# GpSimd instead of VectorE for the weight-block sums, the third-phase operand sums and the input additions

## What is computed

```
q, k, v = x@Wq, x@Wk, x@Wv ;  a = softmax(q k^T / sqrt(512)) v @ Wp + bp
c   = gelu(a@cW1 + cb1)@cW2 + cb2 + onehot(code)          # 512 -> 2048 -> 512
m   = gelu([a, c]@mW1 + mb1)@mW2 + mb2                    # 1024 -> 2048 -> 512
y   = clip(x + c + m, 0, 1)
z   = layernorm(y + gelu(y@Wd[e]+bd[e])@Wu[e]+bu[e])      # expert e of each sequence
```

## Time and profile before

| | |
|---|---|
| median of 3 runs | 1040.34 us |
| the profiled execution, span from its first to its last instruction | 1039.0 us |
| TensorE busy | 1028.9 us, 4857 matmuls |
| VectorE busy | 792.5 us, 1380 instructions |
| ScalarE busy | 524.4 us |
| GpSimd busy | 7.5 us, 18 instructions |
| mean granted TensorE clock | 0.999 of full speed |

### The profile page before, as it was taken

How to read it: one execution, slowest core, us unless ns; L and a number is a source line. 1 busy time by engine, 2 the same in 40 slices (tenths; PEclk the granted TensorE clock), 3 DMA queues, 4 the chain that set the end, 5 groups by cost and what they waited for, 6 DMA issues and landing times.

```text
span 1039.0 us, 13809 instructions
## 1 busy us (share of the span) xinstructions
PE 1028.9 (99%) x4857; PEld 859.5 (83%) x4857; DVE 792.5 (76%) x1380; ACT 524.4 (50%) x955; POOL 7.5 (1%) x18
## 2 busy tenths in 40 slices
PE   8999999999999999999999999999999999999997
PEld 7899888888888878888889888888888887888886
DVE  5647957767598898887966796677668889887798
ACT  4336875454265443433565487554435644434357
POOL 0000000000000000000000000000000000000001
PEclk9999999999999999999999999999999999999999
DMA  8340211210133272521644122312004322423152
GB/s 205 60 183 21 95 48 41 82 41 21 61 144 121 101 201 83 159 85 49 238 120 118 58 68 82 122 41 81 21 21 162 142 81 104 157 98 109 41 163 81
DMA packets 91006, 101.61 MB, mean 98 GB/s; under 512 B 36830, under 2 KB 71738, under 8 KB 87098
## 3 DMA queue, kind: packets, MB, share of 16 engines
q1 hardware_dynamic: 90848, 100.71, 29.8%
q10 hardware_dynamic: 90, 0.02, 0.0%
HBM read 79.74 MB, written 20.97 MB: 97 GB/s over the span
## 4 chain that ended last, share of the span: by engine, by line
PE 59%; DVE 3%; ACT 1%; issue 1%; DVEq 0%; ACTq 0%
PE bank L224 20%; PE bank L225 20%; PE bank L226 20%; DVE acc L1124 0%; PE bank L462 0%; DVE z_last L1281 0%; DVE w_lo L1018 0%; DVE z_last L1290 0%; ACT gel L833 0%; DVE xp2l L1018 0%; ACT acc L810 0%; DVE hid_lo L1018 0%; ACT xp3h L586 0%; ACT e3h L586 0%; PE bank L376 0%
## 5 line engine op out<-in xcount | busy, mean ns | idle before, releaser
L224 PE MATMUL bank<-hid_hi,w_lo 128*128 128x512 f32 x512 | 200.3, 391 | 0.3
L676 ACT ACTIVATE sbc<-sbc,bias 128x512 f32<-128x512 f32 x112 | 80.5, 724 | 236.0 <-DVE sbc L1099 174.4
L225 PE MATMUL bank<-hid_hi,w_hi 128*128 128x512 f32 x512 | 199.3, 389 | 0.0
L226 PE MATMUL bank<-hid_lo,w_hi 128*128 128x512 f32 x512 | 199.2, 389 | 0.0
L1124 DVE TENSOR_TENSOR acc<-bank,acc 128x512 f32<-128x512 f32 x224 | 153.6, 686 | 50.9 <-PE bank L226 50.4
L224 PE MATMUL bank<-ta_hi,w_lo 128*128 128x512 f32 x448 | 174.8, 390 | 0.0
L226 PE MATMUL bank<-ta_lo,w_hi 128*128 128x512 f32 x448 | 174.4, 389 | 0.0
L225 PE MATMUL bank<-ta_hi,w_hi 128*128 128x512 f32 x448 | 174.3, 389 | 0.0
L1099 DVE TENSOR_TENSOR sbc<-bank,sbc 128x512 f32<-128x512 f32 x144 | 98.1, 686 | 38.8 <-PE bank L226 38.6
L586 ACT ACTIVATE sbc<-bank 128x512 f32<-128x512 f32 x112 | 66.4, 595 | 112.7 <-PE bank L226 112.5
L1018 DVE TENSOR_TENSOR w_lo<-w_raw,w_hi 128x256 fp32r<-128x256 f32 (+1 forms) x176 | 93.6, 562 | 37.0 <-ACT w_hi L586 37.0
(11 more groups left out here) (224 smaller groups left out, 1532.4 us busy)
## 6 DMA issues: line engine op xcount, KB each, us to landing
w_raw<-in_L_cond_mW SPq DMA_DIRECT2D x48, 512.0 KB, 3.4
w_raw<-in_L_cond_cW SPq DMA_DIRECT2D x32, 512.0 KB, 4.4
pre_d<-sbc SPq DMA_DIRECT2D x10, 1024.0 KB, 3.9
sbc<-pre_d SPq DMA_DIRECT2D x10, 1024.0 KB, 7.3
x_blk<-in_x SPq DMA_DIRECT2D x64, 64.0 KB, 2.3
e_raw<-in_L_cond_W_down SPq DMA_DIRECT2D x8, 512.0 KB, 4.5
e_raw<-in_L_cond_W_up SPq DMA_DIRECT2D x8, 512.0 KB, 4.1
proj_hi<-aw_hi SPq DMA_DIRECT2D x2, 1024.0 KB, 10.2
```

The source lines that it names most:

```text
L224: nc.tensor.matmul(dst, w_l, a_h, start=start, stop=False, **kw)
L225: nc.tensor.matmul(dst, w_h, a_h, start=False, stop=False, **kw)
L226: return nc.tensor.matmul(dst, w_h, a_l, start=False, stop=stop, **kw)
L676: nc.scalar.activation(dst, dst, ACT.Gelu, **kw).then_inc(g_done[key], 1)
```

## The change

For quads 2 to 23 of each batch the four sums of weight blocks are made by GpSimd (`pool_s`), and so are the four operand sums of phase 3 (`pool_t_sum`) and the two additions of the input (`pool_resid`). Quads 0 and 1 and the operand sums of phase 1 stay on VectorE. GpSimd makes the second of the four sums directly after the first, so that ScalarE waits for two of them (S1 and S2) instead of three. GpSimd's program follows the iterations in an order of its own (`pool_mlp`); its powers for the norms keep their order between the two batches and at the end. The low and high parts are split where they were before.

```diff
@@ -605,7 +605,7 @@
                 act_copy(w1_hi[i % 2][:, 0, :, :], a11).then_inc(w1_h1, 1)
                 act_copy(w1_hi[i % 2][:, 1, :, :], a12).then_inc(w1_h1, 1)
             else:
-                act.wait_ge(s_step, 4 * g + 3)
+                act.wait_ge(s_step, 4 * g + (3 if i < 2 else 2))
                 act_copy(w1_hi[i % 2][:, 2:4, :, :], sf[:, 0:2, :, :]).then_inc(w1_h1, 1)
 
@@ -1128,17 +1128,12 @@
             n0 = 14 * b + 7 * which
             step = 8 * b + 4 * which
             if name == "T1":
-                if which:
-                    dve.wait_ge(evac, 8 * (RB * b + NQ))
-                    dve.wait_ge(w2_l, RB * b + NQ)
-                else:
-                    for e in (0, 1):
-                        dve.wait_ge(ao_done[e], 2 * b + 2)
+                for e in (0, 1):
+                    dve.wait_ge(ao_done[e], 2 * b + 2)
             elif name == "T2":
                 dve.wait_ge(t_step, step + 1)
-                if which == 0:
-                    for e in (2, 3):
-                        dve.wait_ge(ao_done[e], 2 * b + 2)
+                for e in (2, 3):
+                    dve.wait_ge(ao_done[e], 2 * b + 2)
...
-
-        def dve_resid(dve, b, t):
-            if t == 0:
-                dve.wait_ge(t_hi, 14 * b + 14)
-                dve.wait_ge(t_lo, 14 * b + 14)
-                if b:
-                    dve.wait_ge(xr_in, 32 * b)
-                else:
-                    dve.wait_ge(xf_done, 8)
-            dst = acc[:, :, t * TB:(t + 1) * TB]
-            nc.vector.tensor_tensor(dst, dst, xf[:, t, :, :], ALU.add).then_inc(resid_done, 1)
@@ -1433,7 +1417,6 @@
                 dve_c21_pre(dve, b, it - 1)
                 dve_hid(dve, b, it - 1, "11")
                 dve_hid(dve, b, it - 1, "21")
-                dve_s(dve, b, it + 1)
                 dve_s_pre(dve, b, it, 5)
                 dve_s_pre(dve, b, it, 2)
                 dve_w1_first(dve, b, it + 1, (2,))
@@ -1458,22 +1440,15 @@
             if it == 10:
                 dve_t(dve, b, 1, "B11")
                 dve_t(dve, b, 1, "B21")
-                dve_t_sum(dve, b, 1, "T1")
             elif it == 11:
                 dve_t(dve, b, 1, "T1")
                 dve_t(dve, b, 1, "B22")
-                dve_t_sum(dve, b, 1, "T2")
             elif it == 12:
                 dve_t(dve, b, 1, "T2")
-                dve_t_sum(dve, b, 1, "T3")
             elif it == 13:
                 dve_t(dve, b, 1, "T3")
-                dve_t_sum(dve, b, 1, "T4")
             elif it == 14:
                 dve_t(dve, b, 1, "T4")
-                dve_resid(dve, b, 0)
-            elif it == 15:
-                dve_resid(dve, b, 1)
...
-                if 0 < it < QB - 1:
-                    dve_s(dve, b, it + 1)
...
+        def pool_s(pool, b, i):
+            g = quad(b, i)
+            a11, a12, a21, a22 = raw_blocks(i)
+            pool.wait_ge(w1_l1, 3 * g)
+            pool.wait_ge(w1_l2, 2 * g)
+            pool.wait_ge(w1_in[i % 2], 16 * (g // 2) + 16)
+            nc.gpsimd.tensor_tensor(s_f[:, 0, :, :], a21, a22, ALU.add).then_inc(s_step, 1)
+            pool.wait_ge(s_step, 4 * g + 1)
+            nc.gpsimd.tensor_tensor(s_f[:, 1, :, :], s_f[:, 0, :, :], a11, ALU.subtract).then_inc(s_step, 1)
+            nc.gpsimd.tensor_tensor(s_f[:, 2, :, :], a11, a21, ALU.subtract).then_inc(s_step, 1)
+            pool.wait_ge(s_step, 4 * g + 2)
+            nc.gpsimd.tensor_tensor(s_f[:, 3, :, :], a12, s_f[:, 1, :, :], ALU.subtract).then_inc(s_step, 1)
...
+        def pool_t_sum(pool, b, name):
+            a, c = {"T1": ("B12", "B11"), "T2": ("B22", "T1"), "T3": ("B22", "B12"), "T4": ("B21", "T2")}[name]
+            n0 = 14 * b + 7
+            step = 8 * b + 4
+            if name == "T1":
+                pool.wait_ge(evac, 8 * (RB * b + NQ))
+                pool.wait_ge(w2_l, RB * b + NQ)
+            elif name == "T2":
+                pool.wait_ge(t_step, step + 1)
+            elif name == "T3":
+                pool.wait_ge(t_lo, n0 + T_NO["T1"] + 1)
+                pool.wait_ge(t_step, step + 2)
+            else:
+                pool.wait_ge(t_lo, n0 + T_NO["T2"] + 1)
+            nc.gpsimd.tensor_tensor(t_f[:, T_SLOT[name], :, :], t_value(1, a), t_value(1, c), ALU.subtract)\
...
+        def pool_resid(pool, b, t):
...
+            dst = acc[:, :, t * TB:(t + 1) * TB]
+            nc.gpsimd.tensor_tensor(dst, dst, xf[:, t, :, :], ALU.add).then_inc(resid_done, 1)
+
+        def pool_mlp(pool, b):
+            for it in range(1, QB - 1):
+                pool_s(pool, b, it + 1)
+                for name in {10: ("T1",), 11: ("T2",), 12: ("T3",), 13: ("T4",)}.get(it, ()):
+                    pool_t_sum(pool, b, name)
+                if it in (14, 15):
+                    pool_resid(pool, b, it - 14)
+
+        def pool_norm(pool, n, parts):
+            for c, part in parts:
+                pool.wait_ge(ve_done, 2 * n + c + 1)
+                nc.gpsimd.tensor_tensor(rstd[:, part], veps[:, part], mhalf[:, part], ALU.pow).then_inc(rstd_done, 1)
+
         def pool_program(pool):
             nc.gpsimd.memset(ident[:, :], 0.0).then_inc(iotas, 1)
             nc.gpsimd.iota(feat_i[:, :], pattern=[[P, KT]], base=0, channel_multiplier=1).then_inc(iotas, 1)
@@ -1629,11 +1656,13 @@
             pool.wait_ge(consts, 1)
             halves = [slice(2 * h, 2 * h + 2) for h in range(2)]
             singles = [slice(t, t + 1) for t in range(TT)]
-            for n in range(NB - 1):
-                last = (halves[0],) + tuple(singles[t] for _, t in R_TILE)
-                for c, part in enumerate(halves if n < NB - 2 else last):
-                    pool.wait_ge(ve_done, 2 * n + c + 1)
-                    nc.gpsimd.tensor_tensor(rstd[:, part], veps[:, part], mhalf[:, part], ALU.pow).then_inc(rstd_done, 1)
+            for b in range(NBAT):
+                if b:
+                    pool_norm(pool, 2 * b - 2, enumerate(halves))
+                    pool_norm(pool, 2 * b - 1, enumerate(halves))
+                pool_mlp(pool, b)
+            last = (halves[0],) + tuple(singles[t] for _, t in R_TILE)
+            pool_norm(pool, 2 * NBAT - 2, enumerate(last))
```

More of the change, by code:

```diff
@@ new lines, in pool_t_sum @@
+        def pool_t_sum(pool, b, name):
[13 more added lines that the diff above has]
+            nc.gpsimd.tensor_tensor(t_f[:, T_SLOT[name], :, :], t_value(1, a), t_value(1, c), ALU.subtract)\
+                .then_inc(t_step, 1)
@@ new lines, in pool_resid @@
+        def pool_resid(pool, b, t):
+            if t == 0:
+                pool.wait_ge(t_hi, 14 * b + 14)
+                pool.wait_ge(t_lo, 14 * b + 14)
+                if b:
+                    pool.wait_ge(xr_in, 32 * b)
+                else:
+                    pool.wait_ge(xf_done, 8)
+            dst = acc[:, :, t * TB:(t + 1) * TB]
[7 more added lines that the diff above has]
+                    pool_resid(pool, b, it - 14)
```

## The result

The changed kernel takes 1053.76 us (median of 4 runs, 1051.55 to 1055.02) beside 1040.77 for the kernel before (4 runs): ratio 1.0122, 95% interval 1.0106 to 1.0138. Timed again later on another occasion it was 1054.04 for 1040.20, ratio 1.0129 (1.0114 to 1.0145). The change makes the kernel 13 us slower. The forecast was 1045.7, 5.4 us slower, with a range up to 1053: the right direction, and less than half of the size.

What follows compares the result with a forecast made beforehand. TensorE's busy time bounds the kernel, so only its gaps count: 2.98 us of longer chain against 2.83 gained gives +0.15, plus 5.2 for the held port, +5.4 us: 1045.7 us, range 1036.5 to 1053.

Steps and rivals of the forecast that it cites:

- the bound and the places: TensorE busy 1028.9 of 1039.0 us; its small gaps lie at phase 2 borders and in iterations 3 and 18.
- ScalarE's place in line: At phase 2 borders ScalarE copies S1 and S2 before product 4's bank, for which TensorE waits; slack 0.17 us.
- d: Length of one 128x256 addition (a weight sum) on GpSimd, taken as 0.70 us, between 0.42 and 1.28.
- the handing over: In the border chain: VectorE to GpSimd 0.08 us, GpSimd to itself 0.15, GpSimd to ScalarE 0.13.
- the held port: GpSimd's SBUF-reading instructions hold VectorE's two-input ones, mainly in iterations 11, 12, 15: 2.6 us a batch, 5.2 in all.
- the relief: Sums leaving VectorE close its load gaps around iterations 3 and 18; the held port takes back 0.5 us in 18.
- All eight gaps: First batch iteration 18: 0.36, 0.24, 0.52 us; iteration 3: 0.36; second batch 1.06 and 0.29; all counted as gained.
- The sums of quad 2: At the start of phase 1, no longer queued behind VectorE's operands, they can only come earlier; no loss counted.
- the long instructions: GpSimd's phase 3 operand sums, 2.1 us each, and input additions, 3.9 us each, by the factor 1.7 over VectorE.
- long sums: Rival: weight sums on GpSimd take d = 0.95 with the port held in proportion, +14, 1054 us; chance 0.16.
- one way to TensorE: In phase 2 GpSimd's sums delay TensorE through ScalarE's wait for them ahead of the copy from product 4's bank.
- 28 us per us of d: Price of GpSimd's sum length at phase 2 borders, ahead of the bank's copy: 28d - 19.45 us in all.

Runs made afterwards that it cites:

- beside fills: Changed kernel with each input addition replaced by three fills of the same block, which read nothing: 1051.41 us; with two fills 1048.05 us.
- the best move to GpSimd alone: Kernel before with only the weight sums of quads 3 to 10 and 18 to 23 on GpSimd: 1040.55 us, ratio 0.9988.

## Why the prediction was right or wrong

**Right: the bound and the places.** The loss is in the gaps of TensorE, and most of it at the borders of phase 2, through ScalarE's place in line. d is 0.74 us for 0.70, and the handing over is shorter than forecast, 0.24 us in all for 0.36, so that the gaps at the other four borders came out at 0.26 to 0.37 us for 0.30 and 0.37.

**Right: the held port**, and that it is VectorE's instructions with two SBUF inputs that are held, for as long as GpSimd's takes. The Trainium skill (SBUF — State Buffer, "SBUF: two separate sides") has the shared pair of ports as an exclusive lock, which a VectorE instruction with two SBUF inputs takes only against a GpSimd one that reads SBUF. The trace agrees, in its detail too: PSUM-reading instructions stay at 0.69, and beside fills, which read nothing, three low parts take their 1.09.

**Right: the relief.** It was forecast as 2.8 us less 1.0 by the port; iterations 3 and 18 gave 2.0 us. All eight gaps that the prediction named there, 2.8 us, are gone, and two in each batch at the starts of these iterations grew, by 0.8 us together.

**Wrong: "The sums of quad 2 no longer queue on VectorE behind phase 1's operands and can only come earlier."** They came earlier, and that was the harm. At 104.6 instead of after VectorE's operand work, they took turns at the port with that work, and 3.1 us were lost, both batches together; the forecast had 0. I had applied the port to phase 2 and not to the one place where GpSimd's start moved the furthest; quad 2 back on VectorE returned 3.3 to 3.6 us.

**Mis-sized: the long instructions.** "by the same factor 2.1 us for an operand sum and 3.9 for an input addition": undisturbed they take 2.41 and 4.61. The factor is 1.8 for 256 elements and 2.0 for 1024 and 2048: from 256 to 1024 GpSimd's time grows by 1.67 us, 2.2 ns an element, VectorE's by (1.22 - 0.42)/768 = 1.04. And the port works the other way, too, which the prediction left out: an operand sum took 2.87, because it came to the port behind a low part of VectorE's. So what the held VectorE adds to the gaps after iterations 11, 12 and 15, forecast as 0.5, 0.5 and 1.1 us, came to some 1.5, 1.1 and 1.8 in the first batch (0.35 of the 1.5 is GpSimd's late start after iteration 11) and 1.2, 1.1 and 1.8 in the second. Another small piece was left out: S4 holds the low part of S1 and S2 (1.22 us for 0.68), and C12 starts late by that. The borders together gave 11.0 us where 7.2 was forecast. 11.0 + 3.1 - 2.0 is 12.1 of the 13 us; the 5.4 of the forecast were short of it by these 3.8 at the borders and by the 3.1 at the start of phase 1.

The Trainium skill (GPSIMD Engine Reference, "Performance versus the Vector engine") states 4497 ns for an addition of 2048 elements; by it an estimate is 4.5 us for the input addition and 2.2 for the operand sum. The trace agrees within 0.2 us for undisturbed ones, 4.61 and 2.41. The case called long sums in the prediction had nearly the right time, 1054, for a wrong reason, d = 0.95: that is luck.

**Not as I thought: one way to TensorE.** The run with ScalarE's order turned round shows VectorE's lateness by C22 as a second way, so the 28 us per us of d hold only for the order as it stands.

## What to carry to other kernels

GpSimd is not free help for VectorE where both read two tensors from SBUF: until one is through the other waits. VectorE handed over 77 us of work here and was busy only 31.7 us less; for an operand sum it gave away 1.22 us and waited 1.6. The places to look at are those where VectorE's instruction is on the path, and also those where GpSimd, free of VectorE's order, now starts earlier. Before moving work off an engine, ask whether its length or its load is on the path: here the latency of three sums was, and a copy moved ahead of a wait in ScalarE's order gave at least as much (2.1 us) as the best move to GpSimd alone (1.2). Help of this kind paid only in stretches where the result has long to arrive and VectorE is full.

## What was not expected of the hardware

Two streams of instructions that both want the port alternate, one for one, even when GpSimd's follow each other without a wait: between two additions back to back VectorE got in with a single low part, and the next had to wait for the whole second addition, 4.78 us for 0.42. And a long gap of TensorE costs twice: after 5.9 us of standing the granted clock was 0.52 for some 6 us, and low again for about half as long after the same gap in the second batch, while behind the eight gaps of 2.2 us in four traces it stayed at 1.00 seven times and once fell to 0.50 for 3.3 us.
